# Cross attention on one core: the product of the softmax sums in two one-pass products, and a new order of keys and turned queries

## The reference, cut to what matters

```python
q = (hidden_states @ Wq).reshape(B, Sq, H, D)          # x, 512 tokens, H = 16, D = 128
k = (encoder_hidden_states @ Wk).reshape(B, Skv, H, D) # ctx_1024, 512 tokens
v = (encoder_hidden_states @ Wv).reshape(B, Skv, H, D)
q = rmsnorm(q, gq)
k = rmsnorm(k, gk)
scores = jnp.einsum('bqhd,bkhd->bhqk', q, k) * scale
attn = jax.nn.softmax(scores, axis=-1)
out = jnp.einsum('bhqk,bkhd->bqhd', attn, v)
out = out.reshape(B, Sq, H * D)
...
x = _layernorm(x + _L1_xattn_ref(x, ctx_1024, ...), axis=-1)
```

## Time and profile before

| | before |
|---|---|
| median of 3 runs | 2547.98 us |
| profiled execution, its own time | 2548.6 us |
| its span | 2546.8 us |
| PE busy in the span | 2188.1 us (86%) |
| DVE busy | 1422.8 us (56%) |
| ACT busy | 1224.2 us (48%) |
| POOL busy | 932.3 us (37%) |
| granted TensorE clock, mean of the span | 0.948 |

### The profile page before, as it was taken

The page is one execution under the profiler, slowest core; times in us unless marked ns, Lnnn a source line. Parts: engine busy times, 40 slices in busy tenths (PEclk is TensorE's granted clock), DMA queues, the critical chain, the costliest instruction groups (busy, mean ns, idle before and its releaser), DMA issues. The chain is left out here.

```text
span 2546.8 us, 33202 instructions
## 1 busy us (share of the span) xinstructions
PE 2188.1 (86%) x12629; PEld 1551.4 (61%) x12664; DVE 1422.8 (56%) x2129; ACT 1224.2 (48%) x2321; POOL 932.3 (37%) x662
## 2 busy tenths in 40 slices
PE   5989899857896787797999999999999999976781
PEld 4555556436675665555677777777777777753340
DVE  3656666635555435543566665566666655652637
ACT  3636464523424636544555555555555555541413
POOL 2525252410003202203555555555555655520101
PEclk9999999978997999998999999999999999988786
DMA  3000000010001000002111111111111111011001
GB/s 110 1 1 1 1 1 1 1 63 1 1 1 49 1 1 1 1 2 80 47 50 50 58 50 50 42 39 53 50 50 50 50 50 45 20 46 56 1 1 66
DMA packets 60550, 79.12 MB, mean 31 GB/s; under 512 B 6052, under 2 KB 40228, under 8 KB 60392
## 3 DMA queue, kind: packets, MB, share of 16 engines
q1 hardware_dynamic: 60392, 76.99, 9.0%
HBM read 72.78 MB, written 4.19 MB: 30 GB/s over the span
## 5 line engine op out<-in xcount | busy, mean ns | idle before, releaser
L2104 PE MATMUL banks<-s_probsT,s_v 128*128 128x512 f32 x512 | 230.1, 592 | 0.0
L594 DVE TENSOR_REDUCE s_neg_max<-banks 128x1 f32<-128x512 f32 x256 | 165.5, 685 | 89.4 <-PE banks L660 87.9
L2010 DVE RECIPROCAL s_inv_sums<-banks 128x512 f32<-128x512 f32 x64 | 214.2, 3347 | 1.2 <-PE banks L2111 1.2
L1843 POOL TENSOR_TENSOR s_qk_rstd<-s_mean_sq,minus_half 128x8 f32<-128x8 f32 x64 | 105.2, 1643 | 249.2 <-DVE s_mean_sq L1967 246.1
L1936 ACT ACTIVATE s_probsT<-banks,s_minus_bound,s_qk_rstd 128x512 f32<-128x512 f32 x256 | 186.3, 785 | 11.2 <-PE banks L200 11.2
L543 ACT ACTIVATE s_probsT<-banks 128x512 f32<-128x512 f32 x256 | 148.8, 600 | 81.4 <-PE banks L674 79.1
L1964 DVE TENSOR_REDUCE s_mean_sq<-x_cur 128x8 f32<-128x1024 f32 x64 | 78.1, 1220 | 185.5 <-ACT x_cur L1904 174.3
L198 PE MATMUL banks<-s_w_proj_hi,xT_hi 128*128 128x256 f32 x512 | 158.3, 309 | 2.9 <-DVE s_w_proj_lo L1987 2.9
L2104 PEld LDWEIGHTS banks<-s_probsT,s_v 128*128 128x128 f32 x512 | 96.9, 189 | 97.9 <-issue 92.4
L1915 ACT ACTIVATE x_cur<-banks 128x256 f32<-128x256 f32 x128 | 49.3, 385 | 219.3 <-PE banks L200 219.1
L1868 POOL TENSOR_TENSOR x_cur<-s_probsT 128x512 f32<-128x512 f32 x64 | 82.3, 1286 | 193.3 <-ACT s_probsT L1936 193.1
(11 more groups left out here) (417 smaller groups left out, 6156.5 us busy)
## 6 DMA issues: line engine op xcount, KB each, us to landing
s_w_proj_raw<-l1x_wq SPq DMA_DIRECT2D x32, 512.0 KB, 3.3
s_w_out_raw<-l1x_wo SPq DMA_DIRECT2D x32, 512.0 KB, 3.6
s_w_proj_raw<-l1x_wk SPq DMA_DIRECT2D x32, 256.0 KB, 2.8
s_w_proj_raw<-l1x_wv SPq DMA_DIRECT2D x32, 256.0 KB, 3.1
x_all<-x SPq DMA_DIRECT2D x4, 1024.0 KB, 12.7
s_ctxT<-ctxT SPq DMA_DIRECT2D x8, 512.0 KB, 4.9
out<-x_all SPq DMA_DIRECT2D x4, 1024.0 KB, 4.3
s_probsT<-l0a_wqkv SPq DMA_DIRECT2D x1, 1536.0 KB, 9.4
```

What stands on the lines that cost most here:

```text
L594: dve.tensor_reduce(nmax[:, h % 2, t, 0:1], ps.ap(s), AX.X, ALU.max, negate=True) \
L1843: pool.tensor_tensor(rs[:, i, :, :], ms[:, i, :, :], c.mhalf[:, 0:T * HP].rearrange("p (t h) -> p t h", h=HP), ALU.pow).then_inc(rs_ready[ ...
L2010: dve.reciprocal(inv[:, h, :], ps.ap(("SU", j, h))).then_inc(ps.freed(("SU", j, h)), 1)
L2104: mm = pe.matmul(ps.ap(key), v[:, k, h * DX:(h + 1) * DX], probs[:, h, k, :], start=(k == 0), stop=(k == T - 1))
```

## The change

The sums' product is no longer one single precision product. ACT writes a rounded copy of `psum` (SH, 128x512), POOL the rest (SL, 128x512, with a drain behind it), and PE multiplies a rounded matrix of ones with both, in two one-pass products. SH(j,0) and SL(j,0) stand behind E(j,1,1) and OH(j-1,1), SH(j,1) and SL(j,1) behind SU(j,0) in front of R(j,0). So POOL's order becomes U(j,0), SL(j,0), U(j,1), WQ, MQ, SL(j,1), WKl, WOl, MK. U no longer waits for the product of the turn before; SH and SL do.

The order behind V(j,1) becomes KV(j+1,0), KV(j+1,1), TQ(j+1,0), SU(j,1), KV(j+1,2). In the lead-in (j = -1) all four KV stand in front of both TQ. The counters of mean squares and rstd are shared by queries and keys. DVE makes the rounded ones once.

```diff
@@ -1685,6 +1686,9 @@
         f_h = sb("qkT_hi", [P, 2, HP, S], F32R)
         f_l = sb("qkT_lo", [P, 2, HP, S], F32R)
         probs = sb("probsT", [P, HP, T, S])
+        s_h = sb("probs_sum_hi", [P, HP, S], F32R)
+        s_l = sb("probs_sum_lo", [P, HP, S], F32R)
+        ones_r = sb("ones_one_pass", [P, P], F32R)
         inv = sb("inv_sums", [P, HP, S])
         o_h = sb("outT_hi", [P, HP, S], F32R)
         o_l = sb("outT_lo", [P, HP, S], F32R)
@@ -1699,10 +1703,10 @@
         wo_hi, wo_lo = cnt("w_out_hi"), cnt("w_out_lo")
         x_hi, ctx_hi, ctx_lo = cnt("x_hi", KD), cnt("ctx_hi"), cnt("ctx_lo")
         squared = {"q": cnt("q_squared"), "k": cnt("k_squared")}
-        ms_ready = {"q": cnt("q_mean_sq"), "k": cnt("k_mean_sq")}
-        rs_ready = {"q": cnt("q_rstd"), "k": cnt("k_rstd")}
+        ms_ready, rs_ready, nth = cnt("qk_mean_sq", 2), cnt("qk_rstd_ready", 2), {"q": 1, "k": 2}
         q_normed = cnt("q_normed")
         f_hi = {"TK": cnt("kT_hi", HP), "TQ": cnt("qT_hi", HP)}
+        s_hi, s_lo = cnt("sum_hi", HP), cnt("sum_lo", HP)
         p_sum, o_hi, o_lo = cnt("probs_summed", HP), cnt("out_hi", HP), cnt("out_lo", HP)
         var_ready, rstd_ready, nmr_ready = cnt("ln_var"), cnt("ln_rstd"), cnt("ln_shift")
 
@@ -1721,6 +1725,8 @@
                     seq.append(("E", j, 1, k))
                     if prv and k < HP:
                         seq.append(("OH", j - 1, k))
+                    if k == 1:
+                        seq += [("SH", j, 0), ("SL", j, 0)]
                 seq += [("U", j, 1), ("V", j, 0)]
             elif prv:
                 seq += [("OH", j - 1, h) for h in range(HP)]
@@ -1731,7 +1737,7 @@
                     seq.append(("Cx", (j + 1) // G))
                 seq += [("Q", j + 1, 1), ("MQ", j + 1)]
             if now:
-                seq += [("SU", j, 0), ("R", j, 0)]
+                seq += [("SU", j, 0), ("SH", j, 1), ("SL", j, 1), ("R", j, 0)]
             if j + 2 < N:
                 seq.append(("WK", j + 2))
             if now:
@@ -1748,12 +1754,14 @@
                 seq.append(("O", j - 1, 0))
             if now:
                 seq.append(("V", j, 1))
-            if nxt:
-                seq.append(("KV", j + 1, 0))
+            if j < 0:
+                seq += [("KV", 0, 0), ("KV", 0, 1), ("KV", 0, 2), ("KV", 0, 3), ("TQ", 0, 0)]
+            elif nxt:
+                seq += [("KV", j + 1, 0), ("KV", j + 1, 1), ("TQ", j + 1, 0)]
             if now:
                 seq.append(("SU", j, 1))
-            if nxt:
-                seq += [("KV", j + 1, 1), ("TQ", j + 1, 0), ("KV", j + 1, 2)]
+            if nxt and now:
+                seq.append(("KV", j + 1, 2))
             if j + 2 < N:
                 seq.append(("WKl", j + 2))
             if now:
@@ -1761,7 +1769,10 @@
             if prv:
                 seq.append(("O", j - 1, 1))
             if nxt:
-                seq += [("TQ", j + 1, 1), ("KV", j + 1, 3), ("MK", j + 1)]
+                seq.append(("TQ", j + 1, 1))
+                if now:
+                    seq.append(("KV", j + 1, 3))
+                seq.append(("MK", j + 1))
             if prv:
                 seq.append(("O", j - 1, 2))
             if nxt:
@@ -1839,9 +1850,9 @@
         @block.gpsimd
         def _(pool):
             def rstd(i, nm, j):
-                pool.wait_ge(*ms_ready[nm].after(j, 1))
+                pool.wait_ge(*ms_ready.after(j, nth[nm]))
                 pool.tensor_tensor(rs[:, i, :, :], ms[:, i, :, :], c.mhalf[:, 0:T * HP].rearrange("p (t h) -> p t h", h=HP),
-                                   ALU.pow).then_inc(rs_ready[nm].sem, 1)
+                                   ALU.pow).then_inc(rs_ready.sem, 1)
 
             for ph, j, *s in seq:
                 if ph == "WQ" and j > 0:
@@ -1863,13 +1874,18 @@
                 elif ph == "U":
                     h = s[0]
                     pool.wait_ge(*ps.released(0, ("E", j, h, T - 1)))
-                    if j > 0:
-                        pool.wait_ge(*ps.full(0, ("SU", j - 1, h)))
                     pool.tensor_tensor(psum[:, h, :], probs[:, h, 0, :], probs[:, h, 1, :], ALU.add)
                     pool.drain()
                     pool.tensor_tensor(psum[:, h, :], psum[:, h, :], probs[:, h, 2, :], ALU.add)
                     pool.drain()
                     pool.tensor_tensor(psum[:, h, :], psum[:, h, :], probs[:, h, 3, :], ALU.add).then_inc(p_sum.sem, 1)
+                    pool.drain()
+                elif ph == "SL":
+                    h = s[0]
+                    pool.wait_ge(*s_hi.after(j, h + 1))
+                    if j > 0:
+                        pool.wait_ge(*ps.full(0, ("SU", j - 1, h)))
+                    pool.tensor_tensor(s_l[:, h, :], psum[:, h, :], s_h[:, h, :].bitcast(F32), ALU.subtract).then_inc(s_lo.sem, 1)
                     pool.drain()
                 elif ph == "L":
                     pool.wait_ge(*var_ready.after(j, 1))
@@ -1896,11 +1912,17 @@
                 elif ph == "WO":
                     act.wait_ge(*rawo_in.after(j, 16))
                     act.activation(side(wo_h, j), raw_o[:, :], ACT.Copy).then_inc(wo_hi.sem, 1)
+                elif ph == "SH":
+                    h = s[0]
+                    act.wait_ge(*p_sum.after(j, h + 1))
+                    if j > 0:
+                        act.wait_ge(*ps.full(0, ("SU", j - 1, h)))
+                    act.activation(s_h[:, h, :], psum[:, h, :], ACT.Copy).then_inc(s_hi.sem, 1)
                 elif ph == "Q":
                     i = s[0]
                     act.wait_ge(*ps.full(0, ("Q", j, i)))
                     if j > 0:
-                        act.wait_ge(*ms_ready["k"].after(j - 1, 1))
+                        act.wait_ge(*ms_ready.after(j - 1, nth["k"]))
                     sqr = act.activation(sq[:, 2 * i:2 * i + 2, :].rearrange("p a n -> p (a n)"), ps.ap(("Q", j, i)), ACT.Square)
                     if i == 1:
                         sqr.then_inc(squared["q"].sem, 1)
@@ -1911,7 +1933,7 @@
                     kv = ps.ap(("KV", j, t))
                     act.wait_ge(*ps.full(0, ("KV", j, t)))
                     if t == 0:
-                        act.wait_ge(*ms_ready["q"].after(j, 1))
+                        act.wait_ge(*ms_ready.after(j, nth["q"]))
                     sqr = act.activation(sq[:, t, :], kv[:, 0:NW], ACT.Square)
                     if t == T - 1:
                         sqr.then_inc(squared["k"].sem, 1)
@@ -1928,7 +1950,7 @@
                     h, k = s
                     if h == 0 and k == 0:
                         act.wait_ge(bound_ready, 1)
-                        act.wait_ge(*rs_ready["k"].after(j, 1))
+                        act.wait_ge(*rs_ready.after(j, nth["k"]))
                     if k == 0 and j > 0:
                         act.wait_ge(*p_sum.after(j - 1, h + 1))
                         act.wait_ge(*ps.full(0, ("V", j - 1, h)))
@@ -1951,6 +1973,7 @@
         def _(dve):
             def constants():
                 dve.wait_ge(consts, 64)
+                dve.tensor_copy(ones_r[:, :], c.ones[:, :])
                 dve.tensor_tensor(gcol[:, :], gcols[:, 0:1], gcols[:, 1:2], ALU.mult)
                 dve.tensor_tensor(gqk[:, :], gains[:, 0, :], gains[:, 1, :], ALU.mult)
                 dve.drain()
@@ -1965,7 +1988,7 @@
                 dve.drain()
                 per = (1.0 / DX, 1e-5) if nm == "q" else (1.0, 1e-5 * DX)
                 dve.tensor_scalar(ms[:, i, :, :], ms[:, i, :, :], per[0], per[1], ALU.mult, ALU.add) \
-                   .then_inc(ms_ready[nm].sem, 1)
+                   .then_inc(ms_ready.sem, 1)
 
             for ph, j, *s in seq:
                 if ph == "X":
@@ -1987,7 +2010,7 @@
                     dve.tensor_tensor(side(wx_l, 0)[:, OQ:OKV], raw_x[:, OQ:OKV], side(wx_h, 0)[:, OQ:OKV].bitcast(F32),
                                       ALU.subtract).then_inc(wq_lo.sem, 1)
                 elif ph == "NQ":
-                    dve.wait_ge(*rs_ready["q"].after(j, 1))
+                    dve.wait_ge(*rs_ready.after(j, nth["q"]))
                     dve.wait_ge(*ps.released(0, ("Q", j, 1)))
                     x3 = q[:, :, :].rearrange("p t (h n) -> p (t h) n", h=HP)
                     dve.tensor_tensor(x3, x3, rs[:, 0, :, :].rearrange("p t h -> p (t h)").unsqueeze(2)
@@ -2107,8 +2130,11 @@
                 elif ph == "SU":
                     h = s[0]
                     ps.wait_empty(pe, 0, key)
-                    pe.wait_ge(*p_sum.after(j, h + 1))
-                    pe.matmul(ps.ap(key), c.ones[:, :], psum[:, h, :], start=True, stop=True).then_inc(ps.filled(key), 1)
+                    pe.wait_ge(*s_lo.after(j, h + 1))
+                    if j == h == 0:
+                        pe.wait_ge(bound_ready, 1)
+                    pe.matmul(ps.ap(key), ones_r[:, :], s_h[:, h, :], start=True, stop=False)
+                    pe.matmul(ps.ap(key), ones_r[:, :], s_l[:, h, :], start=False, stop=True).then_inc(ps.filled(key), 1)
```

## The result

| | before | after |
|---|---|---|
| median | 2548.03 us (2547.49 to 2548.59, 4 runs) | 2513.05 us (2512.01 to 2514.58, 4 runs) |
| ratio of times | | 0.9863, 95% interval 0.9846 to 0.988 |
| profiled execution's own time | 2548.6 us | 2514.6 us |
| its span | 2546.8 us | 2512.8 us |
| granted TensorE clock, mean of the span | 0.948 | 0.947 |

The forecast was 2559.6 us, slower than before; the kernel became 35 us faster. That is rival A, which stood at 2507. Between the normalisation of the first pair of queries (NQ) and that of the last, where all 31 repeated turns lie, before takes 1046.62 us and after 1011.11 us: 35.51 less. The end of the stage gives about 1.5 us back.

A forecast was written before the change was run, and what follows sets the result against it. PE was taken to set a turn's length. Typical turns +7.6, borders +3.0, turns behind +3.3, first +0.8, last -0.6, lead-in -4.2, end +1.7: +11.6 on 2548.6, median 0.6 lower: 2559.6 us; 8-in-10 range 2505 to 2568.

The forecast's parts named there:

- rival A: In each turn NQ gets the port before POOL's WKl, so every turn gains: 2507 us, chance 0.21.
- Part 3: Copies put on ACT and POOL: WKl starts 0.06 us ahead of NQ, NQ waits, PE stalls 1.9 us a turn.
- the head: Lead-in before the first product E: keys 2 and 3 run while PE waits for NQ; -4.2 us (-3 to -5).
- Both parts of the sum: Sums' product on PE 0.46 us for 0.86, twice a turn; with the new order KV2 1.26 us earlier a turn.
- M: End of DVE's tensor_scalar of the mean squares in a turn: 3.30 us behind SU0's start in place of 2.69.
- both starts: In a turn, POOL's WKl starts at M + 3.12 us and DVE's NQ at M + 3.18 us.
- The exclusion and its price: DVE's NQ and POOL's WKl share a port; the second waits for the whole other: 0 or about 1.8 us a turn.
- The tail: Last turn (j = 31): the last SU1 at 2255.4 and not 2253.27, less 0.40: +1.7 us.
- Rival B: NQ and WKl win the port in turn, as the lead wavers by 0.02 us: about 2533 us, chance 0.08.

## Why the prediction was wrong

**The step that failed** is one sentence of Part 3: "The nearest row is the head ... Hence I take the same here." In the head NQ is released by a semaphore (1.75 us of waiting stand at its row), in a turn it is queued directly behind the reciprocal. I took the lead, 0.07 there and 0.06 here, as what makes the rows alike, and it was not. The leads of all the kernels in which the two came close:

| NQ stands behind | DVE had the port at POOL's lead | POOL had it at |
|---|---|---|
| the reciprocal, a drain in front of POOL's operation | 0.02 to 0.12 | 0.13 to 0.38 |
| the reciprocal, no drain there | -0.03 to 0.08 | 0.09 to 0.28 |
| a small reduction, a drain in front of POOL's operation or WKl (border) | none | 0.04 to 0.28 |
| the subtractions from PSUM of a border | none | 0.00 to 0.35 |
| a semaphore (lead-in, all kernels but the one in which POOL waits) | none | 0.07 |

In before NQ starts 1.48 us or more behind POOL's operation everywhere but in the head, so its trace could not tell who wins a close meeting behind a reciprocal. It did tell the price, 0 or 1.8 us a turn. The odds of 0.65 to 0.21 rested on a single row with another instruction in front.

The Trainium skill, page "SBUF — State Buffer", section "Who interferes with whom", says that the shared port pair is an exclusive lock and that issue order decides who blocks. The traces agree on the exclusion: in the typical turns of after NQ takes its own 1.16 us and WKl 3.43. What they don't bear out is reading that order from the recorded starts, as the prediction did: DVE got the port although it is recorded up to 0.12 us behind.

**What held.** Both parts of the sum: SU0 0.46 us, TQ0, SU1 and KV2 within 0.07, M and both starts within 0.02. The exclusion and its price: in the kernel with NQ 0.15 us later, PE's stall is 1.71 (1.9 worked out) and the turn 33.96 (33.9). The head: 12.70 to 8.30, so -4.4 (-4.2 worked out). The tail, from the last turn's first product E to SU1: 14.67 to 16.75, +2.08 (+2.13, and then 0.40 off). The turn by A: 1.21 less (1.26).

**What was mis-sized in A**, which gave 2507 where 2513 came: the borders. A border and the two periods behind it went from 102.45 to 101.04, 1.41 less, where A counts 1.1 + 1.1 + 1.26 = 3.46. Three times the difference of 2.05 is 6.2 us. Two things make it up. A let NQ win everywhere; at the borders it lost, so NQ took 3.4 us there and PE idled 1.41 us in front of the turned queries. In the kernel in which POOL waits, where NQ wins there too, the same three periods take 99.8, so the lost race is 1.3 of the 2.05. The other 0.8 stay, and A has no term for them: in that kernel too PE waits 0.65 for the low parts of the transposed x, and 0.25 for NQ in the turn behind. That kernel wins 4.9 us back between the first NQ and the last, at the borders and in the lead-in.

**Where the 35 us come from**, then: of the 31 periods from NQ to NQ, the nine at the borders bring 3 x 1.41 = 4.2; the first, in which the head lies, brings 4.4; the other 21 bring 26.9, about 1.2 in a typical turn and more in the second and the last. Together 35.5, as measured. The tail takes back 2.08 less 0.40. That leaves 33.8, of 34.0 between the spans. Rival B (a wavering race) is refuted too: the lead wavers by 0.03 from turn to turn, but the bound is 0.07 away.

**What stays open**: why NQ directly behind a reciprocal gets the port although POOL is recorded ahead, and whether it is the kind of the instruction in front or the moment at which that one began. Only a reciprocal, a small reduction and subtractions from PSUM stood in front here. Shown are the price of the lost race and that NQ wins it in the typical turns; who wins a close meeting is known only for the cases of the table.

## What to carry to other kernels

Where two instructions that exclude each other come to start within some tenths of a microsecond, the order is no property that one can read from the recorded starts: price both outcomes, and make the wanted one certain with a wait on the semaphore that is already there; here that turned a risk of 52 us into 5 us of gain. Look for what is newly behind or in front of each of them, not only for the distance. And work moved into a closed bank's wait is only worth the wait: a shortening of that same work doesn't add to it.

## What the runs showed of the hardware

- Directly behind a reciprocal, a DVE instruction with two SBUF inputs takes the port from a POOL instruction recorded up to 0.12 us ahead (0.08 without a drain in front of POOL's); behind a reduction of 0.09 us, which itself starts behind POOL's, it loses at 0.04. The length of the reciprocal (0.14 or 1.69 us) makes no difference at leads of 0.04 to 0.06.
- Two one-pass products of 512 columns cost 0.46 us where one of single precision costs 0.86, at a granted clock of 1.00.
- A stall of PE of 1.7 us in each turn of 34 us leaves the granted clock at 1.00.
